# Causal attention and gated top-k feed-forward: normed input rows split in float16 halves before they are transposed, by the DMA in place of TensorE

## The chip, the cores and the metric

One core of one Trainium2 chip. The metric is the device time of one execution in microseconds; the median of the runs counts.

## What is computed

Input x is (4, 2048, 512) in float32. Two blocks follow one another:

```
h  = layernorm(x)
q, k, v = relu(h@Wq + bq), relu(h@Wk + bk), relu(h@Wv + bv)
e  = q@k.T / sqrt(512), masked causally;  y = softmax(e) @ v
x1 = x + layernorm(relu(y@Wo + bo))
h2 = layernorm(x1)
out = x1 + layernorm(ffn(h2))
```

In ffn, two gated branches (a grouped convolution, a batch norm over all 8192 rows, gelu, a linear layer, softmax and the largest 32 of 512) choose output and input channels of one 512x512 product. The batch norm needs all rows before any score, so the kernel has two passes.

## The kernel before

All float32 operands of matmuls are split in two float16 halves, hi and lo, and a product is three float16 matmuls (hi*hi, hi*lo, lo*hi), issued by `three` (L444). A tile is 128 rows; a batch has 16 tiles, in 4 groups of 4. The first pass (L342 to L872, up to about 1610 us) runs a loop over the four batches on every engine, each with its own order of work written out by hand and counted semaphores between them. The second pass is the feed-forward part and isn't touched.

A batch has two stages.

*Projections*, for each group g of 512 rows: SP loads the rows tile by tile into `xg` (`load_x`, L352). VectorE takes mean and variance (`ln_stats`, L687), GpSimd the inverse root (`ln_scale`, L881), and VectorE normalises in place (`ln_norm`, L694, behind the second K step of the group before). TensorE's order is in `pe_steps` (L217): four V steps, four K steps, four Q steps of 12 matmuls each, then four `vo` steps of 12 (V times Wo), and one convolution transpose `x`. After each Q step of group g comes an `hT` step (L226) for one tile of group g + 1: four 128x128 float32 transposes of the normed rows into a PSUM bank (`transpose_h`, L469 to L475). ScalarE writes the hi half of the bank to `hT` (`hi_h`, L568, by `hi_half`, L566), scaled by 256, and VectorE the lo half (`lo_h`, L683, by `lo_half`, L681). `hT` has two buffers (L118), both laid over the score buffers `sS`; the first V step of a group waits for the fourth tile's lo half (L493).

*Attention*, over i from 0 to 17 (`attention_steps`, L200): scores of tile i, and for tile u = i - 2 the transposes of its probabilities (`pT`, L520) chunk by chunk and their products with V (`pv`, L528). The four `hT` steps of the next batch's group 0 stand behind the four `pv` steps of the last tile (L210), at i = 17. The `pT` and `hT` steps share two PSUM banks in turn (`take_t`, L451).

Behind attention, three engines finish a tile: `bias_o` (VectorE), `relu_o` (ScalarE), `attention_stats` (VectorE), `attention_scale` (GpSimd), `normed` (ScalarE), `residual` (GpSimd, L898), `residual_stats` (VectorE), `second_scale` (GpSimd, L903), `second_norm` and the convolution (VectorE, L734, L742). They lag by some tiles, so the last tiles of a batch are finished in the next batch's projections: `late_tiles(b, g)`, on VectorE behind the Q steps of group g (L818), on GpSimd behind `ln_scale(b, g + 1)` (L927). GpSimd's part is, for g = 0, attention_scale and residual of the last tile and a second_scale before that, for g = 1 a second_scale, for later groups nothing (L909 to L915).

SP's queue issues all DMAs in the order of its program: in a projection group `late_stores` (L389: the x1 store of the last tile at g = 0, an h2 store at g < 3), then `load_x(b, g + 2)`, then an xc store; in attention the residual's loads and the stores, with `load_x(b + 1, 0)` at i = 15 and `load_x(b + 1, 1)` first thing at i = 17. A load of group g waits until TensorE has transposed the tile that was in its slot (L356).

At the start, ScalarE makes the hi weights of V (L617), then the first four `hT` tiles are done, then the other weights; GpSimd clears a number of buffers (L919 to L921), for which TensorE waits (L483).

Of the kernel before, what the change touches and what calls it, by code (L numbers as in the profile page):

```python
# [25 lines left out]
P = 128  # L26
# [50 lines left out]
def layer_block(nc, x, wqkvo, bqkv, bo, ffw, ffb, linw, linb, convw, chan, ident, negid, mask, out):  # L77
    ctx = ExitStack()
    with ctx:
# [28 lines left out]
        with ExitStack() as actx:  # L108
# [16 lines left out]
            vT = sa("vT", [P, 2, C, 512], F16)  # L125
            ob = sa("ob", [P, 2, D], F32)
# [73 lines left out]
        def attention_steps(i):  # L200
# [16 lines left out]
        def pe_steps():  # L217
            for g in range(GROUPS):
# [14 lines left out]
        def transposes_of(i):  # L233
            return [s for s in attention_steps(i) if s[0] in ("hT", "pT")]

        t_items = [s for s in pe_steps() if s[0] in ("hT", "pT")]
# [5 lines left out]


        t_tail = t_items[t_place["hT", 0]:]

        def t_at(signal, b, step, back=0):


            early = step[0] == "hT" and step[1] < GROUP
            return signal.at(b, t_place[step] - back - (T_ITEMS if early else 0))  # L250
# [15 lines left out]
        t_ps = sig("t_ps", T_ITEMS, late=len(t_tail))  # L266
        t_hi = sig("t_hi", T_ITEMS, late=len(t_tail))
        t_lo = sig("t_lo", T_ITEMS, late=len(t_tail))
# [33 lines left out]
            "act": [t_hi, vkq_ev, vo_hi, p_ok, relu_ok, n_ok, x_ev],  # L302
            "dve": [ln_stat, ln_mv, hn_ok, t_lo, vkq_lo, vo_lo, s_ev, nm_ok, rcp_ok, o_ev, st2_ok,
                    mv2_ok, st3_ok, mv3_ok, h2_ok, pr_ok, xc_ok, bn_ok],
            "pool": [ln_ve, ln_rs, ve2_ok, rsd2_ok, rs2_ok, x1_ok, ve3_ok, rs3_ok],
            "sp": xg_in + xr_in + x1_out + h2_out + xc_out,
# [35 lines left out]
        with nc.Block() as block:  # L342

            @block.sync
            def _(sp):
# [6 lines left out]
                def load_x(b, g):  # L352
                    for j in range(GROUP):

                        if g:
                            sp.wait_ge(t_ps.sem, t_at(t_ps, b, ("hT", GROUP * (g - 1) + j)))  # L356
                        else:
# [5 lines left out]
                            .then_inc(xg_in[j].sem, 16)  # L363

# [32 lines left out]
                for w in (2, 1, 0, 3):  # L397
                    sp.dma_start(w_stage[:, w], wqkvo[w].rearrange("(c p) n -> p c n", p=P)).then_inc(w_in[w], 16)
                load_x(0, 1)
# [10 lines left out]
                with sp.Fori(0, B) as b:  # L410
                    for g in range(GROUPS):
                        late_stores(b, g)
                        if g + 2 < GROUPS:
                            load_x(b, g + 2)
                        store_xc(b, g - 4)
                    for i in range(TILES + 2):
                        if i == TILES - 1:
                            load_x(b + 1, 0)
                        if i == TILES + 1:
                            load_x(b + 1, 1)  # L420
# [6 lines left out]
                        if 0 <= i - 6 < TILES - 4:  # L427
                            store_xc(b, i - 6)
                for g in range(GROUPS):
                    late_stores(B, g)  # L430
                    store_xc(B, g - 4)
                for s in xg_in:
                    sp.wait_ge(s.sem, s.at(B, 1))
                for s in x1_out + h2_out + xc_out:
# [4 lines left out]
            def _(pe):  # L439
# [11 lines left out]
                def take_t(b, step):  # L451

                    pe.wait_ge(t_lo.sem, t_at(t_lo, b, step, 2))
# [15 lines left out]
                def transpose_h(b, step):  # L469

                    t, bank = step[1], take_t(b, step)
                    pe.wait_ge(hn_ok.sem, hn_ok.at(b, t))
                    for c in range(C):
                        mm = nc.tensor.transpose(bank[:, P * c:P * (c + 1)], xg[:, t % GROUP, P * c:P * (c + 1)], idn[:])
                    mm.then_inc(t_ps.sem, 1)  # L475

                for step in t_tail:
                    if step[0] == "hT":
                        transpose_h(0, step)
                    else:  # L480
                        pe.wait_ge(t_ps.sem, t_place[step])
                        pe.sem_inc(t_ps.sem, 1)
                pe.wait_ge(setup_pool, 2)  # L483
                with pe.Fori(0, B) as b:
                    for step in pe_steps():
                        kind, *at = step
                        if kind == "hT":
                            transpose_h(b + 1 if at[0] < GROUP else b, step)
                        elif kind in VKQ:
# [63 lines left out]
            def _(act):  # L553
# [8 lines left out]
                def hi_half(b, step, dst, scale):  # L562

                    act.wait_ge(t_ps.sem, t_at(t_ps, b, step))
                    src = t_bank(step)[:, 0:dst.shape[-1]] if len(dst.shape) == 2 else t_bank(step).rearrange("p (c n) -> p c n", c=C)
                    nc.scalar.activation(dst, src, ACT.Copy, scale=scale).then_inc(t_hi.sem, 1)  # L566
# [42 lines left out]
                def hi_of(b, step):  # L609
                    kind, *at = step  # L610
                    if kind == "hT":
                        hi_h(b + 1 if at[0] < GROUP else b, at[0])
                    else:
                        u, g = at
                        hi_half(b, step, pT[:, chunk_index(u, g) % 2, 0, 0:P * min(GROUP, u + 1 - GROUP * g)], P_SCALE)

                weight_hi(2)  # L617
                for step in t_tail:
                    if step[0] == "hT":
                        hi_h(0, step[1])  # L620
                    else:
                        act.wait_ge(t_hi.sem, t_place[step])
# [819 lines left out]
```

## Time and profile before

| | us |
|---|---|
| median of 3 runs (2361.82 to 2362.25) | 2362.21 |
| the profiled execution's own time | 2362.97 |
| its span, first to last instruction | 2361.0 |
| TensorE busy | 2106.8 |
| VectorE busy | 1600.7 |
| ScalarE busy | 1202.5 |
| GpSimd busy | 905.0 |

The engines in the rows are PE (TensorE, matmul), PEld (its weight loads), DVE (VectorE), ACT (ScalarE), POOL (GpSimd) and SPq (SP's queue, which issues the DMAs). A matmul's duration includes its latency; how fast they follow one another is read from their starts. Busy time of an engine says nothing of the path by itself: idle time of an engine that isn't last in a wait costs nothing. PEclk is the granted clock of TensorE, 1.00 for 2.4 GHz and 0.50 for 1.2 GHz.

### The profile page before, as it was taken

The page shows a single profiled execution, that of the slowest core. Times are in us where ns is not written, and L with a number is a line of the kernel's source. Part 1 is how long each engine was busy: PE and PEld are TensorE (multiplying, and loading weights), DVE is VectorE, ACT ScalarE, POOL GpSimd, SP SyncE. Part 2 cuts the span into 40 slices and gives each one's busy share as a digit, 9 for nine tenths or more (in the row PEclk, how much of TensorE's full clock was granted, in tenths as well). Part 3 has the DMA queues.
Part 4 walks back from the last instruction along what each step waited for, and adds up shares of the span by engine and source line. Part 5 has one row for each costly group of instructions (what it writes and reads, how often), then busy time and mean ns, then how long its engine had stood idle before and what let it go on. Part 6 is the DMA issues. An engine that isn't in the chain of part 4 may idle for free. (4 is left out here: it accounts for less than half of the span.)

```text
span 2361.0 us, 37820 instructions
## 1 busy us (share of the span) xinstructions
PE 2106.8 (89%) x10313; PEld 1027.9 (44%) x10313; DVE 1600.7 (68%) x3574; ACT 1202.5 (51%) x2482; POOL 905.0 (38%) x1126
## 2 busy tenths in 40 slices
PE   6999998999999899989989999983888888888885
PEld 2444454444455444445444444541333343333432
DVE  6544756553665555366655356567999999999994
ACT  4443322444332344423344432324888887888886
POOL 1101211100221100022111012124999998999998
PEclk9999999999999999999999999996999999999998
DMA  4101212100221200021111012122222232222222
GB/s 140 52 10 43 68 59 73 53 26 7 70 67 47 80 30 32 25 70 63 65 42 54 7 48 75 51 84 101 80 84 91 78 96 76 88 86 86 79 93 76
DMA packets 90864, 150.93 MB, mean 64 GB/s; under 512 B 9522, under 2 KB 27058, under 8 KB 90676
## 3 DMA queue, kind: packets, MB, share of 16 engines
q1 hardware_dynamic: 90676, 148.79, 19.5%
q8 instruction: 73, 1.20, 0.2%
q14 instruction: 115, 0.94, 0.1%
HBM read 86.10 MB, written 62.65 MB: 63 GB/s over the span
## 5 line engine op out<-in xcount | busy, mean ns | idle before, releaser
L447 PE MATMUL psum<-work,w_hi 128*128 128x512 f16 x1536 | 459.4, 381 | 9.7 <-DVE w_lo L674 3.7
L447 PE MATMUL psum<-v,work 128*128 128x512 f16 x1632 | 382.2, 385 | 39.1 <-DVE work L681 39.1
L447 PE MATMUL psum<-kT,qT 128*128 128x512 f16 (+3 forms) x1920 | 365.5, 349 | 0.0
L566 ACT ACTIVATE work<-psum 128x512 f16<-128x512 f32 (+2 forms) x228 | 124.3, 551 | 432.3 <-PE psum L526 386.3
L447 PE MATMUL psum<-work,w_lo 128*128 128x512 f16 x768 | 292.3, 381 | 0.0
L681 DVE SCALAR_TENSOR_TENSOR work<-psum,work 128x512 f16<-128x512 f32 (+2 forms) x228 | 144.0, 632 | 214.9 <-ACT work L566 212.9
L581 ACT ACTIVATE work<-psum,bqkv_s 128x512 f32<-128x512 f32 x192 | 131.9, 687 | 265.7 <-PE psum L447 246.4
L905 POOL TENSOR_SCALAR ve<-mv 128x1 f32<-128x1 f32 x66 | 14.6, 221 | 644.5 <-DVE mv L732 644.5
L447 PEld LDWEIGHTS psum<-kT,qT 128*128 128x128 f16 x1920 | 181.8, 98 | 169.7 <-issue 3.6
L447 PEld LDWEIGHTS psum<-v,work 128*128 128x128 f16 x1632 | 158.8, 99 | 221.9 <-DVE work L681 51.1
L1288 DVE MAX8 c<-cut 128x8 f32<-128x512 f32 x384 | 243.9, 674 | 5.6 <-DVE cut L1284 3.9
L447 PEld LDWEIGHTS psum<-work,w_hi 128*128 128x128 f16 x1536 | 150.2, 98 | 181.9 <-issue 9.6
L891 POOL TENSOR_SCALAR ve<-mv 128x1 f32<-128x1 f32 x65 | 15.8, 244 | 489.9 <-DVE mv L725 485.9
L1072 PE MATMUL psum<-fw,xsT 128*128 128x512 f16 x792 | 201.8, 409 | 1.1 <-ACT xsT L1174 1.1
L1072 PE MATMUL psum<-fw,h2T 128*128 128x512 f16 x780 | 180.2, 381 | 0.0
L1284 DVE MATCH_REPLACE8 cut<-c,cut 128x512 f32<-128x512 f32 x256 | 170.5, 671 | 0.0
L447 PE MATMUL psum<-w_hi,vT 128*128 128x512 f16 x512 | 154.9, 379 | 0.0
L591 ACT ACTIVATE ob<-ob 128x512 f32<-128x512 f32 x65 | 40.9, 630 | 174.0 <-DVE ob L717 174.0
L1072 PEld LDWEIGHTS psum<-fw,xsT 128*128 128x128 f16 x792 | 83.2, 105 | 94.9 <-issue 25.0
L704 DVE TENSOR_TENSOR qT<-work,qT 128x512 f16<-128x512 f32 x64 | 44.3, 692 | 115.6 <-ACT qT L582 115.6
L447 PEld LDWEIGHTS psum<-work,w_lo 128*128 128x128 f16 x768 | 75.5, 98 | 91.6 <-issue 1.7
L1072 PEld LDWEIGHTS psum<-fw,h2T 128*128 128x128 f16 x780 | 76.8, 98 | 78.7 <-issue 1.6
(140 smaller groups left out, 3926.5 us busy)
## 6 DMA issues: line engine op xcount, KB each, us to landing
work<-x SPq DMA_DIRECT2D x72, 256.0 KB, 3.1
out<-zn SPq DMA_DIRECT2D x70, 256.0 KB, 3.0
h_scratch<-hb SPq DMA_DIRECT2D x68, 256.0 KB, 2.3
x<-x_scratch SPq DMA_DIRECT2D x66, 256.0 KB, 2.8
x_scratch<-xr SPq DMA_DIRECT2D x65, 256.0 KB, 2.0
h<-h_scratch SPq DMA_DIRECT2D x65, 256.0 KB, 3.7
xr<-x SPq DMA_DIRECT2D x64, 256.0 KB, 2.7
xc_scratch<-xcT SPq DMA_DIRECT2D x68, 128.0 KB, 2.1
```

Of the source, the lines that this page charges most:

```text
L447: mm = nc.tensor.matmul(outp, stat(a), mov(c), start=(n == 0 and k == 0), stop=(n == total - 1 and k == 2))
L566: nc.scalar.activation(dst, src, ACT.Copy, scale=scale).then_inc(t_hi.sem, 1)
L581: nc.scalar.activation(raw[:, n % 2, :], bank, ACT.Relu, bias=bias, scale=QKV_DOWN)
L591: nc.scalar.activation(ob[:, t % 2, :], ob[:, t % 2, :], ACT.Relu).then_inc(relu_ok.sem, 1)
L681: nc.vector.scalar_tensor_tensor(dst, src, scale, hi, ALU.mult, ALU.subtract).then_inc(t_lo.sem, 1)
L704: nc.vector.tensor_tensor(dst[:, 1], raw[:, n % 2, :], dst[:, 0], ALU.subtract).then_inc(vkq_lo.sem, 1)
L891: nc.gpsimd.tensor_scalar(ve2[:], m[:, 1:2], EPS * O_GAIN * O_GAIN, None, ALU.add).then_inc(ve2_ok.sem, 1)
L905: nc.gpsimd.tensor_scalar(ve3[:], mv3[:, t % 2, 1:2], EPS, None, ALU.add).then_inc(ve3_ok.sem, 1)
L1072: mm = nc.tensor.matmul(outp, stat(a), mov(c), start=(fresh and n == 0 and k == 0), stop=(n == total - 1 and k == 2))
L1284: nc.vector.match_replace(dst, eight, src, 0.0).then_inc(top_ok.sem, 1)
L1288: nc.vector.max(dst, src).then_inc(top_ok.sem, 1)
```

## The change

The normed rows of a tile are no longer transposed in float32 by TensorE. They are split while they still lie as rows in `xg`: ScalarE writes the hi half to a new buffer `hhl` and GpSimd the lo half, as rows minus hi half. The scale of 256 goes into the inverse root. Then SP issues two DMA transposes for each tile, of 128x512 float16 (128 KB) each, from `hhl` to `hT`. The `hT` steps leave TensorE's order, and the bookkeeping `t_tail` and `t_at` with them. `hhl` has one slot per tile of a group.

Order: ScalarE's copies for group g + 1 stand behind the four K steps of group g, VectorE's `ln_norm` behind the first K step instead of the second. GpSimd's subtractions stand behind `late_tiles(b, g)`. SP's transposes for group g + 1 stand behind `late_stores(b, g)` and ahead of `load_x(b, g + 2)`. For the next batch's group 0, ScalarE's copies stand at the end of step i = 16, GpSimd's subtractions at the end of i = 16, SP's transposes there too, and `load_x(b + 1, 1)` moves to the end of i = 17. At the start, ScalarE's copies come ahead of the weights and GpSimd's subtractions ahead of its clearing of buffers.

```diff
+            hhl = sa("hhl", [P, GROUP, 2, D], F16)
...
-                    if u == TILES - 1:
-                        yield ("hT", g)
...
-                    if g + 1 < GROUPS:
-                        yield ("hT", GROUP * (g + 1) + c)
...
                         if g:
-                            sp.wait_ge(t_ps.sem, t_at(t_ps, b, ("hT", GROUP * (g - 1) + j)))
+                            sp.wait_ge(h_lo.sem, h_lo.at(b, GROUP * (g - 1) + j))
...
+                def transpose_h(b, g):
+
+                    if g < 2:
+                        last = (TILES - 2, TILES - 1)[g]
+                        wait_apart(sp, t_ps, t_ps.at(b, t_place["pT", last, chunks_of(last) - 1] - T_ITEMS))
+                    else:
+                        wait_apart(sp, vkq_ps, vkq_ps.at(b, vkq_index("q", g - 2, C - 1)))
+                    for j in range(GROUP):
+                        wait_apart(sp, h_lo, h_lo.at(b, GROUP * g + j))
+                        for a in range(2):
+                            sp.dma_start_transpose(hT[g % 2][:, a, :, P * j:P * (j + 1)], hhl[:, j, a, :]) \
+                                .then_inc(hT_in[j].sem, 16)
...
                         late_stores(b, g)
+                        if g + 1 < GROUPS:
+                            transpose_h(b, g + 1)
                         if g + 2 < GROUPS:
                             load_x(b, g + 2)
...
-                        if i == TILES + 1:
-                            load_x(b + 1, 1)
...
+                        if i == TILES:
+                            transpose_h(b + 1, 0)
+                        if i == TILES + 1:
+                            load_x(b + 1, 1)
...
-                        if kind == "hT":
-                            transpose_h(b + 1 if at[0] < GROUP else b, step)
...
                             if kind == "v" and c == 0:
-                                pe.wait_ge(t_lo.sem, t_at(t_lo, b, ("hT", GROUP * g + GROUP - 1)))
+                                for j in range(GROUP):
+                                    pe.wait_ge(hT_in[j].sem, hT_in[j].at(b, g))
...
                 def hi_h(b, t):
                     j = t % GROUP
-                    hi_half(b, ("hT", t), hT[(t // GROUP) % 2][:, 0, :, P * j:P * (j + 1)], W_SCALE)
+                    act.wait_ge(hn_ok.sem, hn_ok.at(b, t))
+                    act.wait_ge(hT_in[j].sem, hT_in[j].at(b, t // GROUP - 1))
+                    nc.scalar.activation(hhl[:, j, 0, :], xg[:, j, :], ACT.Copy).then_inc(h_hi.sem, 1)
...
                         for c in range(C):
                             relu_vkq(b, g, "k", c)
+                            if g + 1 < GROUPS:
+                                hi_h(b, GROUP * (g + 1) + c)
                         for c in range(C):
                             relu_vkq(b, g, "q", c)
-                            if g + 1 < GROUPS:
-                                hi_of(b, ("hT", GROUP * (g + 1) + c))
...
+                        if i == TILES:
+                            for t in range(GROUP):
+                                hi_h(b + 1, t)
...
                             lo_vkq(b, g, "k", c)
-                            if c == 1 and g + 1 < GROUPS:
+                            if c == 0 and g + 1 < GROUPS:
                                 ln_norm(b, g + 1)
                         for c in range(C):
                             lo_vkq(b, g, "q", c)
-                            if g + 1 < GROUPS:
-                                lo_of(b, ("hT", GROUP * (g + 1) + c))
...
-                    nc.gpsimd.tensor_scalar(ve1[:], mv1[:, g % 2, :, 1], EPS, None, ALU.add).then_inc(ln_ve.sem, 1)
+                    nc.gpsimd.tensor_scalar(ve1[:], mv1[:, g % 2, :, 1], EPS, W_SCALE ** -2, ALU.add, ALU.mult).then_inc(ln_ve.sem, 1)
...
+                def lo_h(b, t):
+                    j = t % GROUP
+                    pool.wait_ge(h_hi.sem, h_hi.at(b, t))
+                    nc.gpsimd.tensor_tensor(hhl[:, j, 1, :], xg[:, j, :], hhl[:, j, 0, :], ALU.subtract).then_inc(h_lo.sem, 1)
...
                 ln_scale(0, 0)
+                for t in range(GROUP):
+                    lo_h(0, t)
                 for a in (ob, xr, hb, xcs, xcT, rcp, mv2, mv3, rs2, rs3):
                     nc.gpsimd.memset(a[:], 0.0)
...
                         late_tiles(b, g)
+                        if g + 1 < GROUPS:
+                            for j in range(GROUP):
+                                lo_h(b, GROUP * (g + 1) + j)
...
+                        if i == TILES:
+                            for t in range(GROUP):
+                                lo_h(b + 1, t)
```

## Rows read from the trace of the kernel before

**Rows 1.** The page's part 1: busy time of each engine, share of the span, instructions.

```profile
...
PE 2106.8 (89%) x10313; PEld 1027.9 (44%) x10313; DVE 1600.7 (68%) x3574; ACT 1202.5 (51%) x2482; POOL 905.0 (38%) x1126
...
```

**Rows 2.** Windows: busy us (and instructions) of PE, PEld, DVE, ACT, POOL; PEclk, DMA.

```profile
...
440.00:460.00 20.00, 20.00 (x103) 10.12 (x101) 10.35 (x18) 9.14 (x16) 1.88 (x3) 1.00 0.01 1
1700.00:1720.00 20.00, 15.50 (x75) 6.99 (x73) 20.00 (x46) 18.34 (x40) 18.33 (x18) 1.00 0.28 80
...
```

**Rows 3.** Groups of instructions, by shape: busy us and mean ns; idle before.

```profile
...
L901 POOL TENSOR_TENSOR xr<-ob,xr 128x512 f32<-128x512 f32 x65 | 82.3, 1266 | 71.6 <-ACT ob L596 71.6
...
L474 PE MATMUL psum<-idn,work 128*128 128x128 f32 x272 | 42.6, 282 | 19.9 <-DVE work L697 17.1 <-DVEq L794 2.8
...
L591 ACT ACTIVATE ob<-ob 128x512 f32<-128x512 f32 x65 | 40.9, 630 | 174.0 <-DVE ob L717 174.0
...
```

**Rows 4.** Timeline of PE, group 0 to 1 of batch 1: start us, us.

```profile
...
452.18 0.60 PE L474 MATMUL psum<-idn,work 128*128 128x128 f32 x4
452.62 0.38 PE L447 MATMUL psum<-w_hi,vT 128*128 128x512 f16 x1
...
463.20 0.59 PE L447 MATMUL psum<-work,w_hi 128*128 128x512 f16 x2
...
```

**Rows 5.** Timelines of DVE and POOL at the same place.

```profile
...
454.29 0.68 DVE L681 SCALAR_TENSOR_TENSOR work<-psum,work 128x512 f16<-128x512 f32 x1
...
462.27 1.26 POOL L901 TENSOR_TENSOR xr<-ob,xr 128x512 f32<-128x512 f32 x1
...
```

**Rows 6.** Timelines of PE and POOL, group 1 to 2.

```profile
...
506.60 0.59 PE L447 MATMUL psum<-work,w_hi 128*128 128x512 f16 x2
...
503.31 0.57 POOL L907 TENSOR_TENSOR rs<-ve,expo 128x1 f32<-128x1 f32 x1
...
```

**Rows 7.** Timelines of SP's queue and PE, group 2 to 3.

```profile
...
542.26 0.36 SPq L382 DMA_DIRECT2D h_scratch<-hb  x1
...
550.01 0.59 PE L447 MATMUL psum<-work,w_hi 128*128 128x512 f16 x2
...
```

**Rows 8.** Timelines at batch boundaries (PE, POOL), and a window.

```profile
...
404.60 1.11 PE L526 MATMUL psum<-idn,work 128*128 128x128 f32 x4 [4.67 <-DVE work L681]
405.50 5.18 PE L447 MATMUL psum<-v,work 128*128 128x512 f16 x12
...
411.39 2.75 PE L447 MATMUL psum<-v,work 128*128 128x512 f16 x12
...
419.80 0.59 PE L447 MATMUL psum<-work,w_hi 128*128 128x512 f16 x2 [1.93 <-DVE work L681]
...
795.87 4.56 PE L447 MATMUL psum<-v,work 128*128 128x512 f16 x12
...
402.90 1.26 POOL L901 TENSOR_TENSOR xr<-ob,xr 128x512 f32<-128x512 f32 x1 [1.08 <-ACT ob L596]
...
405.00:411.00 6.00, 6.00 (x21) 2.81 (x20) 2.13 (x5) 0.60 (x1) 1.05 (x3) 0.55 0.46 154
...
```

**Rows 9.** The page's parts 3 and 6, and SP's queue in the timeline.

```profile
...
q1 hardware_dynamic: 90676, 148.79, 19.5%
...
xc_scratch<-xcT SPq DMA_DIRECT2D x68, 128.0 KB, 2.1
...
464.96 2.14 SPq L362 DMA_DIRECT2D work<-x  x4
...
```

**Rows 10.** Timelines of DVE, POOL and PE at the start, and of DVE at 437.

```profile
...
11.22 7.08 DVE L697 TENSOR_SCALAR work<-work,mv,rs 128x512 f32<-128x512 f32 x4 [1.67 <-POOL rs L886]
...
11.13 0.95 POOL L920 MEMSET ob<- 128x1024 f32 x1
...
15.76 0.90 POOL L921 MEMSET bn_all<- 128x960 f32 x1
27.77 0.59 PE L447 MATMUL psum<-work,w_hi 128*128 128x512 f16 x1 [3.70 <-DVE w_lo L674]
437.44 1.91 DVE L697 TENSOR_SCALAR work<-work,mv,rs 128x512 f32<-128x512 f32 x4
...
```

More of the change, by code:

```diff
@@ L233, in transposes_of @@
         def transposes_of(i):
-            return [s for s in attention_steps(i) if s[0] in ("hT", "pT")]
-        t_items = [s for s in pe_steps() if s[0] in ("hT", "pT")]
+            return [s for s in attention_steps(i) if s[0] == "pT"]
+        t_items = [s for s in pe_steps() if s[0] == "pT"]
         m_items = [s for s in pe_steps() if s[0] in ("v", "k", "q", "vo", "s", "x")]
@@ L241, in layer_block @@
         assert T_ITEMS % 2 == 0 and len(m_items) % 4 == 0
[L244 to L250, printed above, removed]
         const_in, bias_in, row_out = sem("const_in"), sem("bias_in"), sem("row_out")
@@ L265, in layer_block @@
         hn_ok = sig("hn_ok", TILES)
-        t_ps = sig("t_ps", T_ITEMS, late=len(t_tail))
-        t_hi = sig("t_hi", T_ITEMS, late=len(t_tail))
-        t_lo = sig("t_lo", T_ITEMS, late=len(t_tail))
+        h_hi = sig("h_hi", TILES)
+        h_lo = sig("h_lo", TILES)
+        hT_in = [sig(f"hT_in{j}", GROUPS, step=32) for j in range(GROUP)]
+        t_ps = sig("t_ps", T_ITEMS)
+        t_hi = sig("t_hi", T_ITEMS)
+        t_lo = sig("t_lo", T_ITEMS)
         vkq_ps = sig("vkq_ps", 3 * TILES)
@@ L433, in _ @@
                     sp.wait_ge(s.sem, s.at(B, 1))
+                for s in hT_in:
+                    sp.wait_ge(s.sem, s.at(B, 0))
                 for s in x1_out + h2_out + xc_out:
@@ L451, in take_t @@
                 def take_t(b, step):
-                    pe.wait_ge(t_lo.sem, t_at(t_lo, b, step, 2))
+                    pe.wait_ge(t_lo.sem, t_lo.at(b, t_place[step] - 2))
                     return t_bank(step)
@@ L467, in conv_transposes @@
                     mm.then_inc(x_ps.sem, 1)
[L469 to L482, printed above, removed]
                 pe.wait_ge(setup_pool, 2)
@@ L562, in hi_half @@
                 def hi_half(b, step, dst, scale):
[L564 to L566 removed]
+                    act.wait_ge(t_ps.sem, t_ps.at(b, t_place[step]))
+                    nc.scalar.activation(dst, t_bank(step)[:, 0:dst.shape[-1]], ACT.Copy, scale=scale).then_inc(t_hi.sem, 1)
                 def hi_h(b, t):
                     j = t % GROUP
[L570 removed]
+                    act.wait_ge(hn_ok.sem, hn_ok.at(b, t))
+                    act.wait_ge(hT_in[j].sem, hT_in[j].at(b, t // GROUP - 1))
+                    nc.scalar.activation(hhl[:, j, 0, :], xg[:, j, :], ACT.Copy).then_inc(h_hi.sem, 1)
                 def relu_vkq(b, g, kind, c):
@@ L609, in hi_of @@
                 def hi_of(b, step):
[L610 to L615, printed above, removed]
-                weight_hi(2)
[L618 to L622, printed above, removed]
-                        act.sem_inc(t_hi.sem, 1)
+                    kind, u, g = step
+                    hi_half(b, step, pT[:, chunk_index(u, g) % 2, 0, 0:P * min(GROUP, u + 1 - GROUP * g)], P_SCALE)
+                for t in range(GROUP):
+                    hi_h(0, t)
+                weight_hi(2)
                 weight_hi(1)
@@ L677, in lo_half @@
                 def lo_half(b, step, dst, hi, scale):
-                    dve.wait_ge(t_hi.sem, t_at(t_hi, b, step))
-                    src = t_bank(step)[:, 0:dst.shape[-1]] if len(dst.shape) == 2 else t_bank(step).rearrange("p (c n) -> p c n", c=C)
-                    nc.vector.scalar_tensor_tensor(dst, src, scale, hi, ALU.mult, ALU.subtract).then_inc(t_lo.sem, 1)
-                def lo_h(b, t):
-                    j, h = t % GROUP, hT[(t // GROUP) % 2]
-                    lo_half(b, ("hT", t), h[:, 1, :, P * j:P * (j + 1)], h[:, 0, :, P * j:P * (j + 1)], W_SCALE)
+                    dve.wait_ge(t_hi.sem, t_hi.at(b, t_place[step]))
+                    nc.vector.scalar_tensor_tensor(dst, t_bank(step)[:, 0:dst.shape[-1]], scale, hi, ALU.mult, ALU.subtract).then_inc(t_lo.sem, 1)
                 def ln_stats(b, g, j):
@@ L774, in lo_of @@
                 def lo_of(b, step):
-                    kind, *at = step
-                    if kind == "hT":
-                        lo_h(b + 1 if at[0] < GROUP else b, at[0])
-                    else:
-                        u, g = at
-                        d = pT[:, chunk_index(u, g) % 2, :, 0:P * min(GROUP, u + 1 - GROUP * g)]
-                        lo_half(b, step, d[:, 1], d[:, 0], P_SCALE)
+                    kind, u, g = step
+                    d = pT[:, chunk_index(u, g) % 2, :, 0:P * min(GROUP, u + 1 - GROUP * g)]
+                    lo_half(b, step, d[:, 1], d[:, 0], P_SCALE)
                 for j in range(GROUP):
@@ L788, in _ @@
                 nc.vector.tensor_scalar(bqkv_s[:], bqkv_s[:], A_SCALE, None, ALU.mult)
-                for step in t_tail:
-                    if step[0] == "hT":
-                        lo_h(0, step[1])
-                    else:
-                        dve.wait_ge(t_lo.sem, t_place[step])
-                        dve.sem_inc(t_lo.sem, 1)
                 weight_lo(0, 2)
@@ L936, in _ @@
                             residual(b, i - 3)
+                        if i == TILES:
+                            for t in range(GROUP):
+                                lo_h(b + 1, t)
                 for g in range(GROUPS):
```

9 lines of the change are left out of this document (5 added, 4 removed).

## The prediction

> **What bounds the kernel now.** I read the profile's page first [rows 1]: of 2361.0 us TensorE is busy for 2106.8 (89%), VectorE for 1600.7, GpSimd for 905.0. Such shares mix stages, so I read windows next [rows 2]: inside a projection stage (440 to 460) TensorE is busy all 20.00 us, ScalarE 9.14 and GpSimd 1.88, so only TensorE counts there; in the second pass (1700 to 1720) VectorE is full instead (20.00 of 20). The change touches nothing in the second pass. Then the groups of instructions [rows 3], for what the removed transposes cost each, and the timelines at the four places where a group of 512 rows starts [rows 4 to 8], because that is where the new transfers must have landed.
>
> **Removed.** The 272 transposes come as 68 sets of four. Inside a projection one set starts at 452.18 and the next matmul at 452.62 [rows 4]: 0.44 us of TensorE's time, with no gap. Three groups per batch have four sets each: 12 x 4 = 48 sets, 48 x 0.44 = 21 us, all on the path, as TensorE has no idle time there. The PSUM copies (ScalarE and VectorE, 0.6 and 0.7 us a tile) lay beside matmuls inside the groups and give nothing more.
>
> **Moved and added.** Per group of four tiles: four copies to float16 on ScalarE (SBUF source; nearest row L591, 0.63 us [rows 3]), four subtractions on GpSimd (nearest row L901, 1.27 us [rows 3], so 5.1 for four), and eight DMA transposes of 128 KB on SP's queue. ScalarE's copies lie in the K steps, where it is half idle: nothing. VectorE's normalisation comes one K step earlier: nothing. GpSimd and SP matter by order. In GpSimd's program the four subtractions stand behind the late tiles of the batch before, and on SP the transposes stand behind the late stores. Behind SP's transposes stand the loads of the group after next and an xc store: the rows are wanted only at the start of the next group, and the V matmuls wait longer for their own tiles than VectorE for these, so nothing. TensorE's first V matmul of the next group waits for all four tiles.
>
> **The price of one transfer.** No row shows a transpose, so I bound it. Below: SP issues four loads in 2.14 us, 0.53 each, and 128 KB land 2.1 us after issue [rows 9]. Above: rows of 128 columns of float16 are pieces of 256 bytes, 512 a transfer, 32 on each of 16 engines; the queue's 90676 packets take 19.5% of 16 engines' 2361 us, 81 ns each (mean 1.6 KB), so 32 cost 2.6 us if small ones cost as much. By bytes alone the same row gives 0.40 us. I take a pitch of 1.2 us, the geometric middle of 0.53 and 2.6, as no row is nearer to one, and as landing of the last 2.1 plus what it moves longer than 0.4, so 2.9. The Trainium skill speaks on both sides: "Advanced Engine Details and Errata", X-Bar Transpose (TRN2), calls such transfers as fast as regular ones, which by the plain rows would be the 2398 us below. "VectorE: DVE Perf Modes", The three transpose paths, gives 1309 ns for one 128x128 block by DMA against 390 ns on TensorE and speaks against the change; taken per block, four in a row, a transfer would cost 5.2 us and the whole would be about 2980 us, an estimate from that page alone. No row decides between them; only TensorE's side is seen here, and at a pace of 0.11 us a block, not 390 ns.
>
> **Group 0 to 1.** VectorE's first late operation follows its last low-half write (454.29 [rows 5]); without that write it comes 0.6 us sooner. It heads the chain of the batch's last tile that ends in GpSimd's residual add, 462.27 to 463.53 [rows 5], so now to 462.9. Only then the subtractions: the first ends at 464.2, the last at 468.0. Eight issues from 464.2 at 1.2: the last at 472.6, landed 475.5. TensorE would start V at 463.20 - 0.43 = 462.8 [rows 4]. Stall 12.7 us.
>
> **Group 1 to 2.** GpSimd's second scale ends at 503.31 + 0.57 = 503.9 [rows 6], now 503.3. Subtractions to 508.4, the first at 504.6; last transfer landed 504.6 + 8.4 + 2.9 = 515.9. TensorE is ready at 506.60 - 0.43 = 506.2 [rows 6]: 9.7 us.
>
> **Group 2 to 3.** GpSimd has no late tile here, but SP stores the last second-norm tile first, at 542.26 [rows 7], now 541.7; transfers from 542.1 land by 553.4, TensorE is ready at 550.01 - 0.43 = 549.6: 3.8 us.
>
> **Clock.** After an idle of 4.67 us, 12 matmuls take 5.18 us (second batch boundary 4.56), against 2.75 at full speed, and the window 405 to 411 shows a granted clock of 0.55, nearly all of it at the lower level of 1.2 GHz [rows 8]: 2.1 us more on average. I charge it at the two long stalls, 4.2 a batch; after an idle of 1.93 us the next matmuls were at full speed (from 419.80) [rows 8], and 3.8 lies between, which I leave uncharged.
>
> **Batch boundary.** TensorE waits there 4.67 us, to 404.60, for a low half of the last tile [rows 8]. ScalarE's four copies now come ahead of its evacuation of that chunk, 2.2 us, so the chunk's pv starts at about 406.8. From there to V before took 419.80 - 405.50 = 14.3; without three sets, one P transpose (now done early), and the 1.93 us wait for the last low half it is 10.6: V at 417.4, 2.4 sooner. GpSimd's subtractions follow the residual add (402.90 to 404.2), transfers from 405.5 land at 416.8: hidden, just. Four boundaries (the last one brings the pass's end forward): 9.6 us. GpSimd's scale of the next tile comes 2 to 3 us later, hidden by TensorE's last tile.
>
> **Start.** V starts at 27.77 [rows 10]. VectorE's four normalisations took 7.08 us beside GpSimd's memsets, 1.91 otherwise [rows 10]; those memsets run from 11.13 to 16.66, 5.5 us. Now they come behind the subtractions (four from 12.5, to 17.6), and TensorE waits for them, to 23.1; and the transfers queue behind 4 MB of weights. I take V at 25.3, 2.5 us gained; bounds 0 and 7.7 (VectorE ready at 20).
>
> **Sum.** Loss 4 x (12.7 + 9.7 + 3.8 + 4.2) = 122. Gain 21 + 9.6 + 2.5 = 33. The profiled execution takes 2362.97 us (span 2361.0), 0.76 above the median 2362.21: 2363.0 + 89 - 0.8 = 2451 us.
>
> **Bounds.** Pitch 0.53, landing 2.2: stalls 7.9, 5.0 and 0, clock 4.2, so 68 - 33 = +35: 2398. Pitch 2.0, landing 3.7: stalls 19.1, 16.1, 10.2, boundary 5.8, clock three times 2.1: 230 - 33 = +197: 2559.
>
> **Rivals.** (A) Transfers priced by packet, 2.6 us: stalls 23.9, 20.9, 15.0, boundary 10.6, clock 8.4, 315 - 33 = +282: 2644. For it: the mean packet; against it: packets there are six times larger. Chance 0.10 for anything above pitch 2.0. The per-block figure of "VectorE: DVE Perf Modes" in the Trainium skill would lie beyond it. (B) Faster. GpSimd's subtraction is much cheaper than L901 because two of its three operands are float16: if it costs 0.45 (VectorE's pace for the same tile, 1.91 / 4 [rows 10]) and transfers go by bytes (0.4, landing 2.1), the stalls are 5.5 and 2.5, 32 us in all if the clock holds; with the start's upper bound the gain is 38: 2356. It decides below 8.2 us of stall a batch. For it: nothing but the smaller type; against it: GpSimd's late chain alone ends when TensorE wants to start, so some stall is certain. 0.05. (C) The same with the start as taken: about 2361, no change. 0.04. (D) The transfer isn't done in blocks but element by element: 65536 elements a transfer, many times my upper end, milliseconds. 0.01; the call is a transpose of its own, which speaks against it. The forecast has 0.80.
>
> **How the numbers follow.** 2451 is the likeliest case. Range 2390 to 2560: from the cheap end of the transfers, a little below, to pitch 2.0; outside it are A, B, C and D, 0.20 (the part of A between 2560 and 2644 is the bound that I leave out). A measurement here tells about 0.2% from no change. Faster 0.05, same 0.04, slower 0.91.
>
> **What would show it.** Right: no transpose line with output in PSUM from the input rows; in each batch TensorE idle ahead of the first V matmul of groups 1, 2 and 3, released by the DMA, longest at group 1; GpSimd's subtraction starting straight after the residual add at group 1 and after the second scale at group 2; a granted clock of half behind the long gaps. The pitch of SP's transposes and their time to landing give my term directly. Wrong: TensorE without a gap at these places (then 2330 to 2340), or gaps at each boundary too (then A).

## The result, and the profile after

| | before | after |
|---|---|---|
| median, us | 2362.2 | 2481.9 |
| profiled execution, span | 2361.0 | 2479.3 |
| TensorE busy | 2106.8 | 2093.3 |
| VectorE busy | 1600.7 | 1560.9 |
| GpSimd busy | 905.0 | 981.0 |
| granted clock, mean | 0.966 | 0.948 |

The change costs 5.1%: ratio 1.0508, 95% interval 1.0489 to 1.0526. The forecast was 2451, its range 2390 to 2560, slower with a chance of 0.91. Where a kernel ran several times, the numbers here and below are from fast runs alone; the one slow run, 3602 us at a granted clock of 0.56, was of the version with both orders first.

The busy times say little, as they did before. The waits say it. From the page's part 5 and the view of waits (engine, line waited for: us in total, times, longest):

```profile
L458 PE MATMUL psum<-work,w_hi 128*128 128x512 f16 x1536 | 480.1, 396 | 154.8 <-DMA work<-hhl 154.8
...
PE psum L458 <- DMA work<-hhl: 154.8, 16, 26.5
```

TensorE waits 154.8 us for the new transfers, in 16 places: the start (26.5, where the kernel before waits as long for other things) and all 15 later starts of a group. The timeline of PE in batch 1 shows four of them; the first row is the attention's last chunk ([rows 8] has its counterpart before), the others are the first V matmuls of groups 0 to 3, which answer to [rows 8], [rows 4], [rows 6] and [rows 7]:

```profile
436.04 4.75 PE L458 MATMUL psum<-v,work 128*128 128x512 f16 x12 [6.67 <-DVE work L672]
...
450.06 0.77 PE L458 MATMUL psum<-work,w_hi 128*128 128x512 f16 x2 [3.43 <-DMA work<-hhl]
...
507.49 1.01 PE L458 MATMUL psum<-work,w_hi 128*128 128x512 f16 x2 [13.93 <-DMA work<-hhl]
...
561.47 1.01 PE L458 MATMUL psum<-work,w_hi 128*128 128x512 f16 x2 [10.05 <-DMA work<-hhl]
...
611.05 1.01 PE L458 MATMUL psum<-work,w_hi 128*128 128x512 f16 x2 [5.35 <-DMA work<-hhl]
```

The other batches repeat these gaps within 0.5 us. What fills the longest one is in the timeline of GpSimd and of SP's queue ahead of group 1:

```profile
492.33 1.27 POOL L881 TENSOR_TENSOR xr<-ob,xr 128x512 f32<-128x512 f32 x1
493.56 4.49 POOL L866 TENSOR_TENSOR hhl<-work,hhl 128x512 f16<-128x512 f32 x4
493.78 0.36 SPq L382 DMA_DIRECT2D x_scratch<-xr  x1
494.40 0.36 SPq L386 DMA_DIRECT2D h_scratch<-hb  x1
495.11 11.02 SPq L366 DMA_TRANSPOSE work<-hhl  x8
506.34 2.01 SPq L353 DMA_DIRECT2D work<-x  x4
```

TensorE had ended its work at 493.56, the very moment at which GpSimd came to the first subtraction. Everything after that is the gap: four subtractions of 1.1 us that run ahead of the queue, eight transposes at 1.4 us each (11.02 for 8), and the landing of the last, 507.49. The issues as a whole, in the view of DMA, have a median of 2.5 us from issue to landing:

```profile
work<-hhl SPq DMA_TRANSPOSE x136, 2.5
```

A ledger made from the first V matmul of each batch and the first score matmul behind its projections (before against after; it adds up to the 118.3 us between the spans):

| stage | after minus before, us |
|---|---|
| start | -1.3 |
| projections, batches 0 to 3 | +30.8, +32.3, +30.3, +31.9 |
| attention with the boundary, three times | +0.7, +1.2, +1.5 |
| last attention and end of the first pass | -2.3 |
| second pass | -6.9 |

In the projections 117.2 us are gaps (13.9 + 10.05 + 5.4 in each of four batches), 48 sets of transposes at 0.44 give 21.1 back, and the rest, 29.2 us, is the lower clock behind the gaps. It is a net number: against 166.7 us for a batch's projections without gaps (batches 2 and 3 of the version with both orders first, below), the change loses about 32 us to the clock, 2.0 behind each of its 16 gaps, and the kernel before some 3 us, in batches 0 and 2. The windows of after show what the clock and the DMA engines do in the gap, and the clock of the ten matmuls behind it (columns as in [rows 2]; the last three are PEclk, DMA share and GB/s):

```profile
495.00:506.00 11.00, 0.00 (x0) 0.00 (x0) 0.00 (x0) 0.00 (x0) 3.04 (x3) 0.64 0.52 119
507.50:511.30 3.80, 3.80 (x10) 1.29 (x11) 1.64 (x4) 0.00 (x0) 0.00 (x0) 0.50 0.92 272
```

The DMA engines are half busy while eight transposes go through: it isn't their bandwidth that sets the 1.4 us. At the head of the first window the two stores are still landing; from 498 to 504, with transposes alone, the share is 0.49.

### The profile page after: what moved, and what is told of

Read it like the earlier page. It is cut to its first block and busy times, and to the rows that moved or that the text cites. A ratio compares the mean times of both kernels' runs of the same rounds, so it can differ in the third digit from the quotient of the medians.

```text
span 2479.3 us, 37144 instructions
## 1 busy us (share of the span) xinstructions
PE 2093.3 (84%) x10041; PEld 996.5 (40%) x10041; DVE 1560.9 (63%) x3506; ACT 1204.7 (49%) x2482; POOL 981.0 (40%) x1194
## 2 busy tenths in 40 slices
DMA packets 164850, 168.75 MB, mean 68 GB/s; under 512 B 83506, under 2 KB 101042, under 8 KB 164660
## 5 line engine op out<-in xcount | busy, mean ns | idle before, releaser
L458 PE MATMUL psum<-work,w_hi 128*128 128x512 f16 x1536 | 480.1, 396 | 154.8 <-DMA work<-hhl 154.8
L458 PE MATMUL psum<-work,w_lo 128*128 128x512 f16 x768 | 302.1, 393 | 0.0
L561 ACT ACTIVATE work<-psum 128x512 f16<-128x512 f32 (+3 forms) x160 | 84.2, 532 | 401.4 <-PE psum L522 401.4
L672 DVE SCALAR_TENSOR_TENSOR work<-psum,work 128x512 f16<-128x512 f32 (+3 forms) x160 | 97.2, 608 | 207.4 <-ACT work L561 207.2
L677 DVE BATCH_NORM_STATS2 st<-work 128x6 f32<-128x512 f32 x68 | 46.0, 677 | 135.3 <-DMA work<-x 134.9
L691 DVE TENSOR_TENSOR vT<-work,vT 128x512 f16<-128x512 f32 x64 | 44.3, 693 | 123.9 <-ACT vT L579 122.6
```

Source lines behind the costliest of these rows:

```text
L458: mm = nc.tensor.matmul(outp, stat(a), mov(c), start=(n == 0 and k == 0), stop=(n == total - 1 and k == 2))
L561: nc.scalar.activation(dst, t_bank(step)[:, 0:dst.shape[-1]], ACT.Copy, scale=scale).then_inc(t_hi.sem, 1)
L672: nc.vector.scalar_tensor_tensor(dst, t_bank(step)[:, 0:dst.shape[-1]], scale, hi, ALU.mult, ALU.subtract).then_inc(t_lo.sem, 1)
L691: nc.vector.tensor_tensor(dst[:, 1], raw[:, n % 2, :], dst[:, 0], ALU.subtract).then_inc(vkq_lo.sem, 1)
```

## The experiments

Theory: the transposes by DMA cost nothing by themselves; what costs is that both links of their chain stand last in two hand-written orders, GpSimd's behind the late tiles and SP's behind the late stores, so that the chain of subtractions and eight transfers (1.4 us each) begins when TensorE is already done. Rivals: the transfers are too slow or disturb the other traffic wherever they stand; or one of the two orders alone decides.

### One order at a time, and both

```diff
-                        late_tiles(b, g)
                         if g + 1 < GROUPS:
                             for j in range(GROUP):
                                 lo_h(b, GROUP * (g + 1) + j)
+                        late_tiles(b, g)
```

> GpSimd's four subtractions ahead of its late tiles; SP's order as in the changed kernel. Theory (each of the three stalls has its own gate: at group 0 to 1 SP's x1 store and the subtractions stand in the way together, at group 1 to 2 only GpSimd, at group 2 to 3 only SP's h2 store): the idle time ahead of the V matmuls stays near 13.9 us in group 1, falls from 10.05 to about 4.7 in group 2, stays 5.3 in group 3; 4 x 5.3, so about 2460 us. Rival (the eight transfers cost what they cost, wherever the subtractions stand): all three gaps stay, 2482 us. Rival (GpSimd's order is the whole matter): all three gaps go, about 2340.

Measured, in one run as for the next three versions: 2466.2 us. SP's queue and PE in batch 1:

```profile
489.05 0.36 SPq L382 DMA_DIRECT2D x_scratch<-xr  x1
489.68 0.35 SPq L386 DMA_DIRECT2D h_scratch<-hb  x1
490.39 11.01 SPq L366 DMA_TRANSPOSE work<-hhl  x8
...
502.75 1.01 PE L458 MATMUL psum<-work,w_hi 128*128 128x512 f16 x2 [13.88 <-DMA work<-hhl]
...
551.41 0.95 PE L458 MATMUL psum<-work,w_hi 128*128 128x512 f16 x2 [4.69 <-DMA work<-hhl]
```

Group 1 waits as long as ever: the transposes stand behind the store of x1, which waits for the residual of the late tile. Group 2 waits 5.4 us less.

```diff
-                        late_stores(b, g)
                         if g + 1 < GROUPS:
                             transpose_h(b, g + 1)
+                        late_stores(b, g)
```

> SP's transposes ahead of the late stores; GpSimd's order as in the changed kernel. Theory: groups 1 and 2 keep their gaps (13.9 and 10.05 us), as the halves come no sooner; the gap of group 3 (5.35 us) goes with its cold matmuls (about 2.2): 4 x 7.5, about 2452 us. Rival (transfers at their price anywhere): 2482. Rival (SP's order is the whole matter): about 2340.

Measured: 2450.96 us. Now group 3 has no gap, group 2 the old one, and group 1 only 0.7 us less, since GpSimd is late:

```profile
499.77 1.01 PE L458 MATMUL psum<-work,w_hi 128*128 128x512 f16 x2 [13.23 <-DMA work<-hhl]
...
554.10 1.01 PE L458 MATMUL psum<-work,w_hi 128*128 128x512 f16 x2 [10.05 <-DMA work<-hhl]
```

With both edits together:

> Both of them together: nothing of the batch before stands ahead of the subtractions or the transposes. Theory: the three gaps per batch go (29.3 us) and with them the time at the lower clock (3 x 2.1), 4 x 35.6 = 142: about 2340 us, under the kernel before. More than the sum of the two single edits (30 + 21 = 51), since each stall needs both. Rival (the transfers slow other traffic, or hold SP so long that the loads come late): gaps stay in part, 2380 to 2450.

Measured: 2333.85 us, 1.2% under the kernel before. Groups 1 to 3 of batch 1 start at 458.17, 499.82 and 541.48 with no gap, and 41.66 us apart, where the kernel before needs 43.40: the transposes' four sets of 0.44. Only group 0 still has its gap at the boundary, 3.39 us to 414.76, and takes 43.41. The transposes still take about 1.4 us each:

```profile
434.11 10.80 SPq L366 DMA_TRANSPOSE work<-hhl  x8
```

They begin 24 us before they are wanted. So the slowness of the transfers is real and costs nothing where they are early. Alone the two edits bring 16 and 31 us, together 148: each order hides behind the other. All three times are within 7 us of what the theory asked for, and both rivals fall. A second timing beside the runs on the boundary:

> The kernel with subtractions and transfers first in the groups, timed again beside the kernel before in three rounds: 2334, ratio 0.988. It is the base against which the two runs with the boundary mended are read.

Measured: 2339.1 us, the middle one of 2337.0, 2339.1 and 2343.4; ratio 0.9908 (0.9884 to 0.9932). The single run of 2334 lay below all three; against this timing the two edits bring 143 us together.

### One transfer for each tile

```diff
-                        for a in range(2):
-                            sp.dma_start_transpose(hT[g % 2][:, a, :, P * j:P * (j + 1)], hhl[:, j, a, :])
+                        sp.dma_start_transpose(hT[g % 2].rearrange("p h c n -> p (h c) n")[:, :, P * j:P * (j + 1)],
+                                               hhl[:, j].rearrange("p h n -> p (h n)"))
```

> The order of the changed kernel, but one transpose of 128x1024 a tile in place of two of 128x512. If a transfer's 1.4 us of pitch is paid per instruction: four issues a group in 5.6 us instead of 11.2, gaps 8.3, 4.5 and 0 us, none at the batch boundary; about 20 us a batch and some clock, near 2390 us. If it is paid per block of columns, on SP's queue or in the DMA engines: one issue takes 2.8 us and the time stays at 2482 us.

Measured: 2405.26 us, with the change's own orders. Twice the columns for the same 1.4 us (5.64 for 4) and a landing of 3.3 us instead of 2.5; the DMA engines' share in the window is 0.94 in place of 0.52 (0.96 from 477 to 481, with the stores ahead of the transposes done). SP's queue, its issues in the view of DMA, PE at group 1, and the window:

```profile
475.27 5.64 SPq L365 DMA_TRANSPOSE work<-hhl  x4
...
work<-hhl SPq DMA_TRANSPOSE x68, 3.3
...
483.02 1.01 PE L457 MATMUL psum<-work,w_hi 128*128 128x512 f16 x2 [9.28 <-DMA work<-hhl]
...
475.00:480.00 5.00, 0.00 (x0) 0.00 (x0) 0.00 (x0) 0.00 (x0) 3.20 (x3) 0.66 0.94 219
```

So at 512 columns the time is a price for each instruction, and at 1024 the engines are as good as full. A still larger transfer would probably bring little; none was run. It missed its 2390 by 15: the gaps of 9.3 and 5.7 us that are left (expected: 8.3 and 4.5) still begin with GpSimd's late subtractions, and each still costs clock.

### The boundary

The change takes 3.4 to 3.9 us at each boundary for the transfers, and the chunk ahead of it waits 6.67 us instead of 4.67. I put the second down to ScalarE's four copies, which delay its copy of that chunk, and moved all three parts forward:

```diff
@@ ScalarE, step i
+                        if i == TILES:
+                            for t in range(GROUP):
+                                hi_h(b + 1, t)
                         if 0 <= u < TILES - 1:
                             relu_o(b, u)
@@ GpSimd, step i
                             ln_scale(b + 1, 0)
+                            for t in range(GROUP):
+                                lo_h(b + 1, t)
@@ SP, step i
+                        if i == TILES + 1:
+                            load_x(b + 1, 1)
                         if 0 <= i - 1 < TILES:
                             load_residual(b, i - 1)
+                        if i == TILES:
+                            transpose_h(b + 1, 0)
```

> Subtractions and transfers first in every group (as in the run with both first), and the batch boundary mended as well: at the last step ScalarE's four copies of the next batch stand ahead of its other work, GpSimd's four subtractions right behind the scaling, SP's eight transposes ahead of the late stores. Theory (what is left at a boundary is the chunk that waits for ScalarE's four copies, 6.67 us idle where the kernel before has 4.67, and 1.8 to 3.4 us for the transfers): about 2.0 + 1.8 to 3.4 saved at each of the three boundaries and 2 at the end of the fourth batch, so 2334 less 14 to 20, about 2316. Rival (the copies and transfers set nothing there; the attention's last chunks and the residual's loads do, so that moving them only delays other work): 2334 or up to 2345, with the idle time at the boundary under another releaser.

Measured: 2330.3 us, ratio 0.9863 (0.9844 to 0.9881): better than both orders alone, but less than the 14 to 20 us that the theory asked for: from the first score matmul to the next batch's V, the three boundaries take 4.9 us less together. The same edit on the change's own orders:

> The changed kernel with the boundary mended alone, groups 0 to 3 in the order of the change. Theory: the same 14 to 20 us as with both mended, so 2482 less that, 2462 to 2468; the stalls ahead of groups 1 to 3 stay at 13.9, 10.05 and 5.4 us. Rival (the time at the boundary is set by something else, or returns as a longer stall in group 1, whose stalls are set by GpSimd and SP): 2478 to 2485.

Measured: 2472.45 us, ratio 1.0467 (1.0448 to 1.0485): 9.5 us gained, between theory and rival (8.2 of them at the three boundaries); the gaps at groups 1 to 3 stayed at 13.9, 10.05 and 5.3, as said. In both the chunk still waits 6.46 us: moving the copies forward together with the subtractions didn't free it. With everything early and one transfer for each tile:

> The order of the run before with one transpose of 128x1024 for each tile in place of two of 128x512. If transfers are hidden everywhere but at the start, only the start moves: four instructions at 1.4 us in place of eight, a few us less, 2310 to 2315 for 2316. If the transfers still bound something in a group or at a boundary, it gains 5 us or more there, 2300 to 2308. If the larger transpose disturbs the loads beside it, it comes out slower than the run before.

> The version with everything early and one transfer per tile, timed again on the same chip as the base of the run beside it: 2322, ratio 0.983.

Measured: 2322.1 us (0.9828, 0.9809 to 0.9848), and on another chip 2321.3 (0.9829, 0.9813 to 0.9845). It gains 8 us on the run with two transfers, where a few at most were expected if the transfers were hidden everywhere: 2.2 at the start, 6.0 at the three boundaries and 1.7 by the clock in group 0 of batch 1, less about 1 us lost elsewhere. At that boundary TensorE is idle 0.28 us ahead of V and group 0 takes 41.73 us; with two transfers it was 2.60 us, and 43.41. These 2.60 us were no wait for the transfers. The last one was issued at 403.3 and they land 2.5 us after issue at most, 8 us ahead of V, and the profile names no releaser (PE, and the view of the tile `hhl` from 390 to 420, of the run with two transfers):

```profile
L366 SPq DMA_TRANSPOSE work<-hhl x8: 1188/1235/1272, 393.6 to 403.3; - x8
DMA to landing us min/median/max: 2.4/2.5/2.5
...
413.82 0.59 PE L458 MATMUL psum<-work,w_hi 128*128 128x512 f16 x2 [2.60 <-issue]
```

So both runs have the transfers hidden at the boundary, and why the one with fewer transfers is idle less there stays open; the idle time stands where TensorE's loop jumps back. The chunk still waits 6.46 us. VectorE's timeline there shows why:

```profile
388.52 2.81 DVE L683 TENSOR_SCALAR work<-work,mv,rs 128x512 f32<-128x512 f32 x4
391.24 1.64 DVE L732 TENSOR_TENSOR prod<-hb,cw_b 128x512 f32<-128x512 f32 x1
392.92 0.69 DVE L735 TENSOR_REDUCE xcs<-prod 128x128 f32<-128x512 f32 x1
```

The normings take 2.81 us instead of 1.91 ([rows 10], the row at 437.44), the product 1.64 instead of 0.68, and the output tile that ScalarE waits for comes 1.9 us later. Beside them run ScalarE's copies and GpSimd's subtractions, both moved there by this edit. To tell them apart, the subtractions went back behind the residual:

```diff
                             ln_scale(b + 1, 0)
-                            for t in range(GROUP):
-                                lo_h(b + 1, t)
...
                             residual(b, i - 3)
+                        if i == TILES:
+                            for t in range(GROUP):
+                                lo_h(b + 1, t)
```

> The version with everything early and one transfer per tile, with one edit: at the boundary GpSimd's four subtractions stand behind its residual again, as in the change. Reason for the run: with everything early, the idle time before the attention's last chunk stayed at 6.46 us, though ScalarE's four copies had gone ahead, since VectorE needed 5.98 us in place of 4.11 from its four normings to the next output tile: the normings took 2.80 us for 1.91, the product behind them 1.64 for 0.68. Theory (GpSimd's subtractions beside them slow VectorE): both return to 1.9 and 0.68 us, the idle time falls to about 4.6 us, the subtractions end some 6 us later and the last transfer lands with them at about 407.5, so that the next batch starts 1 to 2 us earlier: 2316 to 2320 for 2322, or no change if the transfers come last. Rival (ScalarE's copies, which read what VectorE has just written, slow it): the normings stay at 2.8 us and the idle time at 6.4; the run is then 3 to 10 us slower, since the transfers come later and nothing is given back.

Measured: 2318.7 us, ratio 0.9818 (0.9802 to 0.9835). The same rows, GpSimd's subtractions, and the chunk:

```profile
388.85 1.91 DVE L683 TENSOR_SCALAR work<-work,mv,rs 128x512 f32<-128x512 f32 x4
390.67 0.68 DVE L732 TENSOR_TENSOR prod<-hb,cw_b 128x512 f32<-128x512 f32 x1
...
396.38 5.15 POOL L865 TENSOR_TENSOR hhl<-work,hhl 128x512 f16<-128x512 f32 x4
396.86 5.17 PE L457 MATMUL psum<-v,work 128*128 128x512 f16 x12 [4.60 <-DVE work L671]
...
399.00 1.52 DVE L732 TENSOR_TENSOR prod<-hb,cw_b 128x512 f32<-128x512 f32 x1
```

With the copies still beside them the normings are back at 1.91 and the chunk waits 4.60 us: it was GpSimd. Now the product at 399.00 runs beside the subtractions, and it is that one that takes 1.52. The slowing is mutual (5.15 for four subtractions, 4.49 alone). In the change itself the subtractions lie clear of the normings, and there the copies do hold the chunk by 2 us, as its timeline of ScalarE shows: the write that the chunk waits for stands behind them, at 434.68, which is 405.31 on the clock of the kernel before, where it is at 403.23.

```profile
432.60 2.18 ACT L567 ACTIVATE hhl<-work 128x512 f16<-128x512 f32 x4
434.68 1.07 ACT L561 ACTIVATE work<-psum 128x512 f16<-128x512 f32 x2
```

So the chunk has two possible makers of its wait: move copies and subtractions both, and the subtractions take the place of the copies. This is the fastest version of all, 1.8% under the kernel before; against the run beside it (2321.3) the intervals overlap, so the last 2.6 us are likely but not certain.

### The second pass

Its code is untouched, yet from VectorE's first to its last maximum over scores (`MAX8 m<-psum`) it takes 693.9 us before and 686.8 after; the expectations below have 694.5 for the first. VectorE, full there [rows 2], sets it, and most of the difference lies at the loop's jump back. Part 5 has it in the group's idle time, the kernel before first:

```profile
L1288 DVE MAX8 c<-cut 128x8 f32<-128x512 f32 x384 | 243.9, 674 | 5.6 <-DVE cut L1284 3.9 <-issue 1.7
```

```profile
L1276 DVE MAX8 c<-cut 128x8 f32<-128x512 f32 x384 | 244.1, 675 | 0.0
```

The 5.6 us are seven stops, one behind each of the seven jumps. The longest in the timeline of before, beside the same place of after, where only the stop of 2.0 us at the jump itself is left (the seven make 5.6 of the 7.1 us):

```profile
1984.28 0.09 DVE L1284 MATCH_VALUE_LOAD cut<-e,ex 128x8 f32 x1 [2.16 <-issue]
...
1987.35 1.29 DVE L1288 MAX8 c<-cut 128x8 f32<-128x512 f32 x2 [1.66 <-issue]
```

```profile
2106.45 0.09 DVE L1272 MATCH_VALUE_LOAD cut<-e,ex 128x8 f32 x1 [2.04 <-issue]
2106.53 0.68 DVE L1272 MATCH_REPLACE8 cut<-e,ex 128x512 f32<-128x512 f32 x1
```

If it is only where the code lies, small instructions ahead of the loop must move it, in the kernel before:

```diff
                 nc.vector.memset(ones[:], -A_SCALE)
+                for i in range(8):
+                    nc.vector.memset(pad[:, 2 * i:2 * i + 2], 0.0)
```

> The kernel before with eight more small memsets on VectorE ahead of the second pass, some 0.5 us of work, and no other edit. The second pass, which the change does not touch, is 7 us shorter in every version of the changed kernel, and the difference sits at the first instructions behind the loop's jump, where the kernel before is idle 1.66 us once more. Theory (where the loop's code lies decides how often VectorE waits for instructions behind the jump): the second pass comes out near 687 or at some other length than 694.5 us, total 2355 or so. Rival (the difference comes from the changed data path, its tiles' places or what the first pass leaves): 694.5 us again, total 2362.

> As the run before with twenty memsets, about 1 us of work. Theory: the second pass differs from that of the kernel before in one of the two runs at least (687 in place of 694.5 us). Rival: 694.5 us in both.

Measured: 2368.2 and 2358.0 us in one run each, beside 2361.1; the second pass 700.1 and 686.1 us. Both runs have the same extra tile and differ only in the number of memsets, so it isn't the places of the tiles. With eight, each of the seven jumps has a second stop:

```profile
1897.30 0.09 DVE L1287 MATCH_VALUE_LOAD cut<-e,ex 128x8 f32 x1 [2.05 <-issue]
1899.34 0.69 DVE L1287 MATCH_REPLACE8 cut<-e,ex 128x512 f32<-128x512 f32 x1 [1.95 <-issue]
```

With twenty, there is one stop a jump. All versions of the changed kernel lie between 685.6 and 688.2 us. So some 7 us of the change's result come from where the code happens to lie, not from what it does: net of them it costs about 127 us, and some 7 of the 43 us of the best version come from there too. The kernel before has one profiled run and each shifted version one run, so the size is no better known than that.

## Why the prediction was right, and where its terms were off

The forecast held by its mechanism: late subtractions behind the late tiles, late transfers behind them, TensorE idle at the first V matmul of groups 1 to 3, longest at group 1. The chain's places were met closely. Laid over the kernel before (the batch starts 30.26 us later), GpSimd's first subtraction comes at 463.3 (predicted 462.9) and TensorE is ready at 463.3 (462.8). It came out 31 us low, by these terms (in us over the whole run):

| term | predicted | measured |
|---|---|---|
| gaps at groups 1 to 3 | +104.8 | +117.2 |
| clock behind them | +16.8 | +29.2 |
| transposes removed | -21 | -21.1 |
| boundaries and end of the first pass | -9.6 | +1.1 |
| start | -2.5 | -1.3 |
| second pass | 0 | -6.9 |
| sum | +88.5 | +118.2 |

Part of the nearness is luck: the second pass's 6.9 us, which the forecast didn't have, hid some of the miss; without them the sum is 37 us low.

**The price of one transfer**: "I take a pitch of 1.2 us", between 0.53 and 2.6. It is 1.4, which adds 7 x 0.2 = 1.4 us to each chain; the landing of 2.5 for 2.9 and a subtraction of 1.1 for 1.27 give some back. The upper bound was made of 81 ns for a packet. The transposes brought 73984 packets under 512 bytes (83506 for 9522), 544 for each transfer; from 498 to 504, with transposes alone, the queue has

```profile
q1 hardware_dynamic: 2379, 0.58, 48.5%
```

so that one packet has 0.485 x 6 x 16 / 2379 us = 20 ns of engine time, and one transfer 10.6 us. The price by packet (A) was four times too high. The Trainium skill, "Advanced Engine Details and Errata", X-Bar Transpose (TRN2), has these transfers as fast as regular ones; the trace disagrees on how fast they follow one another at 512 columns, 1.4 us against 0.53 for a load of twice the bytes [rows 9], while the landing of 2.5 us is near the 2.1 of a plain store of 128 KB [rows 9]. The Trainium skill, "VectorE: DVE Perf Modes", The three transpose paths, has 1309 ns for one block, which as an estimate would be 5.2 us for the four blocks of a transfer: the trace disagrees as well, since one transfer of four or of eight blocks takes 1.4.

**Clock**: "I charge it at the two long stalls, 4.2 a batch". Its size for one stall was right, about 2.1, but it is paid four times a batch, at group 3 and at the boundary too (8.3 us in batch 1, once its gaps and the removed transposes are taken off). "3.8 lies between, which I leave uncharged" chose the wrong side. In the runs, group 0 took 41.75 us behind a gap of 1.87 us (both orders first, batch 2), and 43.41 behind 2.60 and behind 3.39 us. The length of the gap alone doesn't decide it: of the two runs with memsets, batch 2 began at a granted clock of 0.51 (3.3 us of it) behind 2.02 us with eight, and at 1.00 behind 2.34 us with twenty.

**Batch boundary**: "V at 417.4, 2.4 sooner". It came about 1 us later. TensorE's side was right: on the clock of the kernel before (29.37 us less, by VectorE's last output tile) the chunk starts at 406.7 (predicted 406.8) and TensorE is ready for V at 417.3 (417.4). But "hidden, just" was wrong: I had the last transfer landed at 416.8, and it landed at 420.7. The first began 0.9 us later than I took it (435.78, so 406.4), eight took 1.4 us more by their pitch, and the last landed some 4.4 us after its issue, not 2.9; why it lands later there than in the groups (2.5) isn't shown. The fourth boundary, the end of the first pass, gave 2.3 of its 2.4.

**Start**: 1.3 of 2.5 gained. **Second pass**: "the change touches nothing" there, true of its code and not of its time.

The signs that the prediction asked for were all there, and one that it named for its rival A too: gaps at each boundary. They came at a pitch of 1.4, by a first transfer issued later and a last one landing later than forecast, not at a pitch of 2.6.

## What to carry to other kernels

When work moves from an engine that computes to one that sends, what matters is its place in each hand-written order that it passes, here GpSimd's and the queue's: either alone repaired gave 16 and 31 us, both some 145. Put the transfers ahead of whatever waits for late results, and count the lower clock behind each new gap of TensorE on top, about 2 us here behind gaps of 3.4 us and more. And before a difference of 0.3% is put down to a change, look whether a loop that it doesn't touch has changed too.

## What the runs showed of the hardware beyond what was expected

- A DMA transpose inside SBUF costs 1.4 us on SP's queue with 512 and with 1024 columns of float16; the DMA engines are 0.49 and 0.96 busy meanwhile, the landing takes 2.5 and 3.3 us, and that of the last one at a boundary 4.1 to 4.5.
- GpSimd's subtraction of 128x512 (float32 rows, float16 result) slows VectorE's norming (1.91 to 2.81 us for four) and product (0.68 to 1.64) beside it, and is slowed (4.49 to 5.15); beside the same subtractions VectorE's reduction stays at 0.69. ScalarE's copies did nothing of the kind.
- At a loop's jump back VectorE stops for 2.0 us, and once more, up to 2.2 us, in some placements of the code: the same second pass took 686, 694 and 700 us in the three placements of the kernel before that ran. Why the stop comes twice isn't known from these runs. TensorE too is idle up to 2.6 us behind its jump with no releaser in the profile (0.28 in the same place of another version).
